# A Mamba block and a ternary feed-forward on one core: convolution as scaled copies summed on GpSimd, Silu in one activation, high parts on GpSimd, new step tables

## What is computed

```python
xx, res = split(x @ in_w.T)                       # 512 channels each
xx  = silu(causal_conv(xx, 4 taps) + conv_b)      # per channel
delta, B, C = split(xx @ xproj_w.T)
delta = softplus(delta @ dt_w.T + dt_b)
state = exp(delta * A) * state + delta * B * xx   # 16 states per channel, along the tokens
y   = sum_n(state * C) + xx * D
x   = layernorm(x + (y * silu(res)) @ out_w.T)
h   = silu(lin1(x)) * lin2(x)                     # 1024 hidden
h   = gelu(linh1(h)); h = gelu(linh2(h))          # 1024 x 1024 each
x   = layernorm(x + lin3(h))
```

## Time and profile before

| | |
|---|---|
| median of 3 runs | 3148.1 us (3145.47 to 3153.55) |
| profiled execution | 3155.72 us, its span 3153.9 us |
| PE busy | 2583.1 us, 82% |
| DVE busy | 2621.1 us, 83% |
| ACT busy | 2343.3 us, 74% |
| POOL busy | 1071.0 us, 34% |
| granted clock of TensorE, mean | 0.897 |

### The profile page before, as it was taken

The page is one execution under the profiler, slowest core; times in us unless marked ns, Lnnn a source line. Parts: engine busy times, 40 slices in busy tenths (PEclk is TensorE's granted clock), DMA queues, the critical chain, the costliest instruction groups (busy, mean ns, idle before and its releaser), DMA issues.

```text
span 3153.9 us, 41504 instructions
## 1 busy us (share of the span) xinstructions
PE 2583.1 (82%) x12290; PEld 1944.8 (62%) x12290; DVE 2621.1 (83%) x2625; ACT 2343.3 (74%) x3653; POOL 1071.0 (34%) x1028
## 2 busy tenths in 40 slices
PE   4355788888888888988888898888888889898888
PEld 1223566676666666676666766666676756666666
DVE  3678998989898897989889898988989898998830
ACT  2776687877969787796968779697877969687822
POOL 0112333333433433343343334234333423423432
PEclk8566899999989999999989999899999989899999
DMA  1996787787878778787887878787787878778933
GB/s 52 290 321 140 167 193 180 185 197 184 194 179 193 190 181 186 183 194 183 190 188 179 194 181 194 179 196 189 178 190 181 200 186 196 189 180 191 229 111 110
DMA packets 230192, 585.49 MB, mean 186 GB/s; under 512 B 26016, under 2 KB 26400, under 8 KB 229808
## 3 DMA queue, kind: packets, MB, share of 16 engines
q0 software_dynamic: 73728, 268.47, 46.2%
q1 hardware_dynamic: 119344, 246.86, 22.4%
q10 hardware_dynamic: 36864, 67.13, 7.9%
HBM read 281.93 MB, written 31.98 MB: 100 GB/s over the span
## 4 chain that ended last, share of the span: by engine, by line
PE 32%; DVE 29%; ACT 17%; issue 14%; DMA 4%; ACTq 1%; DVEq 1%; SPq 1%; POOL 1%; POOLq 0%
PE ffn_ps L479 17%; DVE scan_ps L782 11%; DVE hC L792 5%; PE scan_ps L367 5%; ACT dB L616 4%; ACT dA L607 3%; DVE y L806 3%; PE misc_ps L372 3%; DMA x<-ffn_w 3%; PE misc_ps L423 2%; DVE gate L899 2%; PE misc_ps L460 2%; PE misc_ps L408 2%; ACT L607 2%; PE misc_ps L367 2%
## 5 line engine op out<-in xcount | busy, mean ns | idle before, releaser
L782 DVE TENSOR_TENSOR_SCAN scan_ps<-dA,scan_ps 128x1024 f32<-128x1024 f32 x512 | 1170.8, 2287 | 57.0 <-PE scan_ps L367 33.2
L968 POOL DMA_DIRECT2D y<-hC x512 | 446.1, 871 | 1811.2 <-DVE hC L792 1735.1
L367 PE MATMUL scan_ps<-ident,dB 128*128 128x128 f32 x4096 | 613.4, 300 | 375.7 <-DVE hC L792 292.3
L367 PEld LDWEIGHTS scan_ps<-ident,dB 128*128 128x128 f32 x4096 | 519.9, 154 | 521.2 <-DVE hC L792 305.5
L616 ACT ACTIVATE dB<-duT,bT 128x512 f32<-128x512 f32 x1024 | 726.4, 711 | 154.5 <-PE scan_ps L367 153.2
L607 ACT ACTIVATE dA<-delta,a_neg 128x512 f32<-128x512 f32 (+1 forms) x1024 | 710.1, 712 | 41.1 <-DVE hC L792 38.0
L479 PE MATMUL ffn_ps<-hb_hi,ring 128*128 128x512 f32 x1536 | 660.1, 430 | 18.4 <-DVE gate L899 8.7
L792 DVE TENSOR_TENSOR hC<-scan_ps,c_rows_sb 128x1024 f32<-128x1024 f32 x512 | 623.6, 1218 | 49.8 <-DMA y<-hC 41.5
L479 PE MATMUL ffn_ps<-hb_lo,ring 128*128 128x512 f32 x1536 | 620.7, 404 | 0.0
L479 PE MATMUL ffn_ps<-ha_hi,ring 128*128 128x512 f32 x1024 | 443.5, 433 | 2.4 <-POOL ha_lo L990 2.4
L479 PE MATMUL ffn_ps<-ha_lo,ring 128*128 128x512 f32 x1024 | 407.7, 398 | 0.0
(11 more groups left out here) (90 smaller groups left out, 2941.9 us busy)
## 6 DMA issues: line engine op xcount, KB each, us to landing
y<-hC POOLq DMA_DIRECT2D x512, 512.0 KB, 5.8
ring<-split_weights SPq DMA_DIRECT2D x704, 256.0 KB, 4.3
c_rows_sb<-c_rows ACTq DMA_DIRECT2D x256, 256.0 KB, 4.0
xt<-x_tok SPq DMA_DIRECT2D x32, 512.0 KB, 6.1
x<-ffn_w SPq DMA_DIRECT2D x22, 512.0 KB, 9.7
split_weights<-ha_hi SPq DMA_DIRECT2D x22, 512.0 KB, 5.2
split_weights<-ha_lo SPq DMA_DIRECT2D x22, 512.0 KB, 7.0
out_tok<-out_st SPq DMA_DIRECT2D x16, 512.0 KB, 2.9
```

Source lines behind the costliest of these rows:

```text
L367: mm = nc.tensor.transpose(dst[:, j * P:(j + 1) * P], src(j), ident[:])
L782: nc.vector.tensor_tensor_scan(b, dA[:, a:a + 2, :].rearrange("p a l -> p (a l)"), b, 0.0, ALU.mult, ALU.add).then_inc(scan_done, 1)
L968: pool.dma_start(y2[:, par, c:c + 2, :], hC[:, p % 2], accum_op=ALU.add).then_inc(y_added[p % 2], 16)
```

## The change

The convolution's taps become three more scaled copies on ScalarE, into buffers that are idle then (`tap_of`: parts of `delta2` or `du`), and three additions on GpSimd. `misc_ps` is free when the copies are made. Both silus are one activation `Silu`, which is a third table; the four of the convolution are taken together at step 39 (`F_U`). Softplus takes abs and relu on ScalarE straight from PSUM, with the bias; the sum of relu and exp goes to GpSimd (`base_step`), and VectorE's bias and maximum operations are gone. The high parts are copies on GpSimd, right before the subtraction (`split_tile`). `x1` has two buffers; all step tables are new; the scratch of GpSimd's DMA descriptors is set to 8192 bytes.

```diff
-F_XT, F_XX, F_DBL, F_DBL_OUT, F_BT, F_BT_OUT = (26, 28), (30, 32, 34, 36), 39, 40, 45, 46
...
+T_GATE = (3, 5, 8, 10)
+T_OUT = (13, 15, 16, 17)
...
+E_W3 = (11, 12, 15, 16)
...
+GELU_AT = (37, 38, 39, 47, 47, 48, 51, 51, 58, 58, 59, 67, 68, 68, 72, 72)
+SPLIT_AT = (39, 42, 43, 47, 47, 49, 52, 52, 59, 60, 63, 69, 69, 71, 74, 74)
+F_U = 39
...
+F_XX = (29, 31, 34, 35)
...
+F_DT = (42, 43, 45, 47)
...
-NO_EXP = {s % TILES for s in GELU_AT}
...
+NO_EXP = {s % TILES for s in GELU_AT} | {F_U} | set(T_GATE)
...
                     c = F_XX.index(s)
                     if c:
-                        pe.wait_ge(conv_taps, r * (DC * (TAPS - 1)) + c * (TAPS - 1))
+                        pe.wait_ge(conv_base, r * (DC * TAPS) + c * TAPS)
...
+                    if t == 2:
+                        wait_past(pe, gelu_x32, r * (2 * HC))
...
                 if s - 1 in F_XX:
                     c = F_XX.index(s - 1)
                     act.wait_ge(pe_xx, r * DC + (c + 1))
-                    nc.scalar.activation(y2[:, par, c, :], misc_ps[:], ACT.Identity, bias=conv_half[:, c, TAPS:],
-                                         scale=conv_half[:, c, TAPS - 1:TAPS]).then_inc(conv_base, 1)
-                if s - 2 in F_XX:
-                    c = F_XX.index(s - 2)
-                    act.wait_ge(conv_taps, r * (DC * (TAPS - 1)) + (c + 1) * (TAPS - 1))
-                    nc.scalar.activation(delta2[:, par, c, :], y2[:, par, c, :], ACT.Tanh).then_inc(u_tanh, 1)
+                    nc.scalar.activation(y2[:, par, c, :], misc_ps[:], ACT.Identity, bias=ch[:, c, C_CONVB:C_CONVB + 1],
+                                         scale=ch[:, c, TAPS - 1:TAPS]).then_inc(conv_base, 1)
+                    if c >= 2:
+                        act.wait_ge(conv_taps, r * (DC * (TAPS - 1)) + (c - 1) * (TAPS - 1))
+                    for back in range(1, TAPS):
+                        tap = TAPS - 1 - back
+                        nc.scalar.activation(tap_of(par, c, back)[:, 0:SEQ - back], misc_ps[:, 0:SEQ - back], ACT.Copy,
+                                             scale=ch[:, c, tap:tap + 1]).then_inc(conv_base, 1)
+                if s == F_U:
+                    for c in range(DC):
+                        act.wait_ge(conv_taps, r * (DC * (TAPS - 1)) + (c + 1) * (TAPS - 1))
+                        nc.scalar.activation(y2[:, par, c, :], y2[:, par, c, :], ACT.Silu).then_inc(u_ready, 1)
...
-                for c in range(DC):
-                    if F_EXP[c] != s:
-                        continue
-                    act.wait_ge(dt_ready, r * DC + (c + 1))
-                    nc.scalar.activation(du[:, c, :], delta2[:, par, c, :], ACT.Abs).then_inc(sp_abs, 1)
+                if s - 1 in F_DT:
+                    c = F_DT.index(s - 1)
+                    act.wait_ge(pe_dt, r * DC + (c + 1))
+                    nc.scalar.activation(du[:, c, :], misc_ps[:], ACT.Abs, bias=ch[:, c, C_DTB:C_DTB + 1]
+                                         ).then_inc(sp_abs, 1)
+                    nc.scalar.activation(delta2[:, par, c, :], misc_ps[:], ACT.Relu, bias=ch[:, c, C_DTB:C_DTB + 1]
+                                         ).then_inc(dt_ready, 1)
                     act.wait_ge(sp_abs, r * DC + (c + 1))
                     nc.scalar.activation(du[:, c, :], du[:, c, :], ACT.Exp, scale=-1.0).then_inc(sp_exp, 1)
...
-                    nc.scalar.activation(gate[:, c % 2, :], misc_ps[:], ACT.Tanh).then_inc(v_tanh, 1)
+                    nc.scalar.activation(gate[:, c % 2, :], misc_ps[:], ACT.Silu).then_inc(v_ready, 1)
...
-                if A_L1 + A_HI <= s < A_L1 + A_HI + HC:
-                    o = s - A_L1 - A_HI
-                    act.wait_ge(l1_x32, f * HC + (o + 1))
-                    nc.scalar.activation(ha_hi[:, o, :], x32[:, o % X32, :], ACT.Copy).then_inc(ffn_hi, 1)
...
-                if s - 1 in F_XX:
-
-                    c = F_XX.index(s - 1)
-                    for back in range(1, TAPS):
-                        if back == 1:
-                            dve.wait_ge(conv_base, r * DC + (c + 1))
-                        else:
-                            dve.wait_ge(conv_taps, r * (DC * (TAPS - 1)) + (c * (TAPS - 1) + back - 1))
-                        tap = TAPS - 1 - back
-                        nc.vector.scalar_tensor_tensor(
-                            out=y2[:, par, c, back:], in0=misc_ps[:, 0:SEQ - back], scalar=conv_half[:, c, tap:tap + 1],
-                            in1=y2[:, par, c, back:], op0=ALU.mult, op1=ALU.add).then_inc(conv_taps, 1)
-                if s - 2 in F_XX:
-                    c = F_XX.index(s - 2)
-                    dve.wait_ge(u_tanh, r * DC + (c + 1))
-                    nc.vector.scalar_tensor_tensor(out=y2[:, par, c, :], in0=delta2[:, par, c, :], scalar=1.0,
-                                                   in1=y2[:, par, c, :], op0=ALU.add, op1=ALU.mult
-                                                   ).then_inc(u_ready, 1)
-                if s - 1 in F_DT:
-                    c = F_DT.index(s - 1)
-                    dve.wait_ge(pe_dt, r * DC + (c + 1))
-                    nc.vector.tensor_scalar(delta2[:, par, c, :], misc_ps[:], ch[:, c, C_DTB:C_DTB + 1], None,
-                                            ALU.add).then_inc(dt_ready, 1)
...
-                for c in range(DC):
-                    if F_MAX[c] != s:
-                        continue
-                    dve.wait_ge(sp_lost, r * DC + (c + 1))
-                    nc.vector.scalar_tensor_tensor(out=delta2[:, par, c, :], in0=delta2[:, par, c, :], scalar=0.0,
-                                                   in1=du[:, c, :], op0=ALU.max, op1=ALU.subtract).then_inc(sp_max, 1)
+                    dve.wait_ge(sp_base, r * DC + (c + 1))
+                    nc.vector.scalar_tensor_tensor(out=delta2[:, par, c, :], in0=sp_w[c], scalar=1.0,
+                                                   in1=delta2[:, par, c, :], op0=ALU.subtract, op1=ALU.subtract
+                                                   ).then_inc(sp_lost, 1)
...
+            def conv_step(r, par, s):
+                if s - 2 in F_XX:
+                    c = F_XX.index(s - 2)
+                    for back in range(1, TAPS):
+                        pool.wait_ge(conv_base, r * (DC * TAPS) + (c * TAPS + back + 1))
+                        if back > 1:
+                            pool.wait_ge(conv_taps, r * (DC * (TAPS - 1)) + (c * (TAPS - 1) + back - 1))
+                        nc.gpsimd.tensor_tensor(y2[:, par, c, back:], y2[:, par, c, back:],
+                                                tap_of(par, c, back)[:, 0:SEQ - back], ALU.add).then_inc(conv_taps, 1)
+
+            def base_step(r, par, s):
+                for c in range(DC):
+                    if F_BASE[c] != s:
+                        continue
+                    pool.wait_ge(dt_ready, r * DC + (c + 1))
+                    pool.wait_ge(sp_exp, r * DC + (c + 1))
+                    nc.gpsimd.tensor_tensor(delta2[:, par, c, :], delta2[:, par, c, :], du[:, c, :], ALU.add
+                                            ).then_inc(sp_base, 1)
...
-            def low_tile(f, i):
-
+            def split_tile(f, i):
+
+                if i < HC:
+                    pool.wait_ge(l1_x32, f * HC + (i + 1))
+                else:
+                    if i == 2 * HC:
+                        pool.wait_ge(pe_half, f * HALVES + 2 * HC)
+                    pool.wait_ge(gelu_x32, f * (2 * HC) + (i - HC + 1))
+                hi, lo = (hb_hi, hb_lo) if HC <= i < 2 * HC else (ha_hi, ha_lo)
+                pool.sem_inc(split_begun, 1)
+                nc.gpsimd.tensor_copy(hi[:, i % HC, :], x32[:, i % X32, :]).then_inc(ffn_hi, 1)
                 pool.wait_ge(ffn_hi, f * FFN_TILES + (i + 1))
-                hi, lo = (hb_hi, hb_lo) if HC <= i < 2 * HC else (ha_hi, ha_lo)
                 nc.gpsimd.tensor_tensor(lo[:, i % HC, :], x32[:, i % X32, :], hi[:, i % HC, :].bitcast(F32),
                                         ALU.subtract).then_inc(ffn_lo, 1)
```

142 lines of the change are left out of this document (74 added, 68 removed).

## The result

The changed kernel takes 3026.3 us (median of 4 runs, 3019.27 to 3032.54), the one before 3149.4 beside it: ratio 0.9608, 95% interval 0.9584 to 0.9633, 3.9% faster. The profiled execution took 3025.48 us with a span of 3023.3 and a granted clock of 0.919.

The account below looks back on a forecast made before the run. VectorE was taken to bound A (47.1 + 2.3 = 49.4 us), ScalarE B to D (119.7 + 5.8 = 125.5): 174.9 us an iteration for 181.5, saving 99 us less 4 at the front; 3053 us, range 2945 to 3140.

Parts of the forecast that it names:

- The 4 us for the first row's front: Before iteration 0: late additions, three silus and two table loads make the first row's front about 4 us longer, once.
- A: Steps 16 to 31 of an iteration: still bound by VectorE, 47.1 us plus 2.3 above it, 49.4 us.
- B to D: Steps 32 to 63 and 0 to 15: now bound by ScalarE, 119.7 us plus 5.8 of waits, 125.5 us.
- the waits that were kept in the sum: ScalarE's waits for TensorE in B to D, 3.5 + 2.3 = 5.8 us, taken as unchanged.
- VectorE's relief: VectorE loses 18.6 us in B to D, from 113.1 to 94.5, leaving it 30 us of room.
- TensorE's work in A: One input and two output projections move there from B to D: 38.4 + 5.5 = 43.9 us.
- The high parts: ScalarE loses 24 copies at 0.622 us an iteration, 16 of them (10.0 us) in B to D.
- The tables: New step tables move one input projection (1.88 us) and two output projections (3.62 us) from B and D to A.
- 4 us are covered: GpSimd's queue may delay the additions of `hC` 4 us: VectorE wants them after 11 us, issue and transfer take 7.
- The rival of a stopped scan: GpSimd's queue delays the additions of `hC` and VectorE's scan: 10.4 us more an iteration, 3308 us; chance 0.12.
- the rival of the dearer switch: Silu's table switches each bring 1.4 us of emptying, 8.2 us for six: 3176 us; chance 0.03.
- The signs of being wrong: VectorE waiting over about 30 us for additions, scaled copies or Silu over 0.7 us, or `misc_ps` stalls making B longer.

Follow-up runs that it names:

- the last kernel: Changed kernel with both layer normalisations moved from VectorE to ScalarE and a row's two end residual additions to GpSimd: 38 us slower than the changed kernel.

## Why the prediction was right, and where it wasn't

- **The number.** 3053 was forecast with 2945 to 3140; 3026 was measured. The step of the sum that is off most is the base of the difference. The sum set the new iteration, 174.9, against the one that was taken apart, 181.5, though the earlier trace rows gave a mean of 183.2. The new period is 174.6, so the new iteration was right to 0.3 us, and the saving was 8.6 an iteration where 6.6 was counted: 129 us for 99. The 4 us for the first row's front didn't come: its base copies follow every 6.2 to 6.4 us where they did every 7.0.
- **A.** 49.4 forecast, 49.6 in the mean. VectorE has 47.2 (47.1 forecast). That it is the bound is shown by both kernels that put work there, 6.6 us for 6.2 and 2.1 for 2.0. It doesn't follow that taking work away pays: the last kernel took 2.8 us away and lost 1.8.
- **B to D.** 125.5 forecast, 125.4 in the mean; ScalarE 119.7 forecast, 118.2 measured. That the sum fits to 0.1 us is partly luck: ScalarE's time is 1.5 us less than forecast and its idle time 1.4 more, and the waits that were kept in the sum, 5.8 us for TensorE, came to 2.9 (`duT` 2.5, `y` 0.4), the rest being others, such as 1.8 before the Gelus. The reason, "bound by ScalarE", fell: 6.7 us less of it there gave 1.2 with the rest of the kernel as it was. Nor does TensorE alone hold them (11.7 us for 2.5), nor VectorE, nor the DMA. What 5.8 us of kept waits stood for is a list of waits between TensorE, ScalarE and GpSimd, with TensorE and ScalarE each 7 to 10 us below the length; the sum of busiest engine and its known waits measured that length well and named its cause badly.
- **VectorE's relief** of 18.6 us in B to D was counted as nothing there. It is worth little, but perhaps not nothing: 23.2 us put back cost 3.9, a sixth.
- **TensorE's work in A** was to grow from 38.4 to 43.9 us, and is 38.6. The steps were read as if they lay in the stretch of their number. But TensorE works off its list apart from VectorE's scans, by which the stretches are cut: in the iteration shown A already held 16 of the 32 matmuls of the output projections before, and holds 24 now, so that one moved and not two; and it holds 64 transposes of the scan for 72. B to D have 115.6 for "at most 113.6". The number wasn't in the sum, since A is VectorE's.
- **The high parts** were priced as 10.0 us of ScalarE. Taken back they cost 20.5 us an iteration in this order of work. The hand-over from ScalarE to GpSimd, and for a part that wasn't separated the later subtractions of stage A, are what the sum left out.
- **The tables** were read as moves of single projections. The three of the feed-forward alone are worth 86 of the 123 us once the other parts are in; the prediction gave the places of Gelus and halves no term of their own.
- **GpSimd.** 115 us forecast, 99.6 measured: copies at 0.68 to 0.80 for 1.0, the subtraction at 1.28 for 1.49. Its queue has less room than "4 us are covered" says: 25 us more in it cost 5.3. The rival of a stopped scan didn't come: VectorE did wait 13.3 us for the additions, but halving the transfers, which left 2.2 of 10.2 us of this wait in the mean, gained only 1.5. With more work in the queue the low parts ahead of TensorE get late as well, which the rival didn't name.
- **Table loads**, 19 an iteration as forecast, cost 1.30 to 1.32 us each with what lies around them, so the rival of the dearer switch falls.
- **The signs of being wrong.** The scaled copies take 0.70 us and Silu 0.60 to 0.62, within the 0.7 that was set; B is shorter than before, and the wait for the additions is under 30 us.

What is shown is the cause in A, and for B to D what the single parts are worth when they are taken back. What holds B to D at their present length, and which of the hand-overs one would have to shorten next, stays open.

## What to carry to other kernels

When several engines are within a tenth of a stretch's length, test each with a little work more and a little less before calling one the bound: here 8 additions in A cost nearly their full time, and 6.7 us less of the busiest engine of B to D gave 1.2. Try the two halves of a hand-over that follow each other (copy and subtraction) on one engine: here the copy takes no longer on GpSimd than 0.68 to 0.80 us, for 0.62 on ScalarE, and the subtraction no longer waits for another queue. Before work is moved off the bound engine, count the chain that it stands in: here taking 2.8 us from the bound engine put 5 us of new waits for ScalarE and GpSimd into its list.
